# Turning an expert tile's rows by transposing DMAs instead of by PE transposes and an ACT copy

## The chip, the cores and the metric

The kernel runs on one core of one Trainium2 chip. The metric is the device time of one execution in microseconds. The kernel before takes 1347.95 us, the median of three runs (1347.94 to 1348.74).

## The reference, cut to what matters

The input is 16 images of 256 channels by 16 x 16 pixels. Two blocks follow each other. Each is a small gated or plain 1x1 convolution and then a mixture of experts over the 4096 pixels ("tokens") of 256 channels:

```python
# block 0, per token, over the top 2 of 8 experts (H = 512)
h = xf @ w1[e].T ;  g = xf @ w3[e].T ;  out += comb * ((silu(h) * g) @ w2[e].T)
# block 1, per token, over the top 2 of 8 experts (F = 1024)
h = silu(xf @ w1[e] + b1[e]) ;  out += comb * (h @ w2[e] + b2[e])
```

Both act on layer-normed tokens, and a router (a softmax over 8 logits) picks two experts for each token.

## The kernel before, in words

The kernel calls the two mixtures f = 0 and f = 1. Each is done sparsely. A token that chose expert e stands as one row in that expert's list; the lists are cut into tiles of 256 rows, so 8192 rows and their padding give 35 tiles here. Before a mixture the layer-normed rows are written to HBM (`rows_x`), each as 512 f16 numbers, 256 "high" parts and 256 "low" parts. `bounds[e]` holds the first tile of expert e; each engine loads all nine of its values into registers (`value_load`) and runs a loop per expert from `edges[e]` to `edges[e+1]`.

Around one tile n the engines do this:

* **POOL** (`feed_experts`, lines 446 to 494): `fetch_next` copies the list of row numbers and issues two indirect gathers (line 432), each bringing 128 rows to `x_rows`, [128 tokens, 512] f16. `put` copies the list of targets and issues two indirect scatters (line 471) of `y_rows` to HBM. `after(n, ...)` is a loop of one pass, written so that a wait can use the loop's own counter.
* **PE** (`experts`, line 718): `up` multiplies the tile's columns `x_cols` (channels on the partitions) by the expert's first weights, 48 matmuls of 256 columns for either f. `down` multiplies the activated result by the second weights, 24 matmuls in all for f = 0 (two calls of 12) and 48 for f = 1 (four calls of 12). Each product is formed from three f16 products (`PARTS`). Between the second-last and the last `down` stands `turn_rows(f, n + 1)` (line 675): 8 PE transposes of 128 x 128 f16 that turn the next tile's `x_rows` into a PSUM bank.
* **ACT** (line 869) applies Silu, makes the f16 parts for f = 0, and in `columns16` (line 863) copies the turned bank into `x_cols`, one instruction of 1024 columns a tile. For f = 0 it also moves the output to `y_rows`.
* **DVE** multiplies, forms the low parts and, for f = 1, moves the output to `y_rows`. For f = 0 it also finds, after each expert, the peaks of one expert's weights of mixture 1 (`scan1_peaks`), which lie in `scan1`.
* **SP** issues the loads of those weights, `load_scan`, two of 1 MB for each expert (lines 308 and 310): two experts' weights as soon as mixture 0's own weights are in place (`w_lo[0]`), then one more each time that DVE has finished one (`scanned`).

`x_rows` and `x_cols` exist once each. The order is kept by semaphores: `xr_loaded` (rows gathered), `xr_turned` (the bank is turned, which also frees `x_rows`), `xc_ready` (columns in place), `z_ready` (an `up` half is done, four a tile), `y_copied` and `y_free` (output moved, output stored). As the PE turns the next tile only after the last `up` of this one, `x_cols` is free when ACT writes it.

Of the kernel before, what the change touches and what calls it, by code (L numbers as in the profile page):

```python
# [24 lines left out]
ALU = mybir.AluOpType  # L25
# [3 lines left out]
F16 = mybir.dt.float16  # L29
# [21 lines left out]
def bass_metaformer(nc, x, conv_w, conv_b, gn_w, gn_b, gate0, w1, w2, w3, weight, bias,  # L51
                    gate1, gate1_b, v1, b1, v2, b2, out):
    ctx = ExitStack()
    with ctx:
# [214 lines left out]
        v1_scaled, v1_lo, fac_ready = sem("v1_scaled"), sem("v1_lo"), two("fac_ready")  # L269
        xr_loaded, xr_turned, xc_ready = two("xr_loaded"), two("xr_turned"), two("xc_ready")  # L270
        z_ready, silu_done, hid_ready, hi_ready, lo_ready = two("z_ready"), two("silu_done"), sem("hid_ready"), two("hi_ready"), two("lo_ready")
# [7 lines left out]
        def _(sp):  # L279
# [94 lines left out]

            sp.wait_ge(moves_ready[1], 1)
            total = sp.value_load(bounds[0:1, E:E + 1], min_val=E, max_val=TILES)
            sp.wait_ge(y_free[1], 32 * total + 16)
# [5 lines left out]
        def _(pool):  # L383
# [44 lines left out]

            def fetch(f, row_lists):

                for g_ in range(2):
                    nc.gpsimd.indirect_dma_start(x_rows[:, g_, :], None, rows_x[f],  # L432
                                                 bass.IndirectOffsetOnAxis(ap=row_lists[g_], axis=0)
                                                 ).then_inc(xr_loaded[f], 16)

# [10 lines left out]
            def feed_experts(f):  # L446


                if f == 0:
                    pool.wait_ge(peak_ready, E)  # L450
                    spread_peaks(0)
                pool.wait_ge(moves_ready[f], 1)
                pool.wait_ge(rows_stored[f], 16 * HB)
                total = pool.value_load(bounds[0:1, E:E + 1], min_val=E, max_val=TILES)
                fetch(f, [first_rows[:, g_:g_ + 1] for g_ in range(2)])
# [24 lines left out]

                fetch_next(0)
                with pool.Fori(0, total) as n:
                    fetch_next(n + 1)
                    put(n)

                def all_done(m):
                    pool.wait_ge(xc_ready[f], m + 2)
                    pool.wait_ge(xr_loaded[f], 32 * m + 96)
# [39 lines left out]
        def _(pe):  # L528
# [143 lines left out]

            x_turn16 = turn[0][:].bitcast(F16).rearrange("p (k s n) -> p k s n", k=KC, s=2)

            def turn_rows(f, tile):

                pe.wait_ge(xr_loaded[f], 32 * (tile + 1))
                for k in range(KC):
                    for s_ in range(2):
                        for r in range(2):  # L680
                            last = pe.transpose(x_turn16[:, k, s_, r * P:(r + 1) * P],  # L681
                                                x_rows[:, r, s_ * C + k * P:s_ * C + (k + 1) * P], ident16[:])
                last.then_inc(xr_turned[f], 1)

            PARTS = ((0, 0), (0, 1), (1, 0))

            def up(f, e, h):

                ws = ((w1_s, zb[2 * (h % 2)]), (w3_s, zb[2 * (h % 2) + 1])) if f == 0 else ((v1_s, zb[h]),)
                for w, z in ws:  # L690
                    for c in (2 * h, 2 * h + 1):
                        to = z[:, (c % 2) * TILE:(c % 2 + 1) * TILE]
                        for k in range(KC):
                            for ws_, xs_ in PARTS:
                                last = pe.matmul(to, w[:, e, k, ws_, c * P:(c + 1) * P], x_cols[:, k, xs_, :],  # L695
                                                 start=(k == 0 and ws_ + xs_ == 0), stop=(k == KC - 1 and ws_ == 1))
                    last.then_inc(z_ready[f], 1)
# [20 lines left out]
            def experts(f):  # L718
# [20 lines left out]
                if f == 1:  # L739
                    pe.wait_ge(xc_ready[1], edges[E] + 1)  # L740

# [48 lines left out]
        def _(act):  # L790
            def deviation(s):
                act.wait_ge(var_ready[s], 1)
                r, v = (rstd[:], var[:]) if s < 4 else (rstd_gn, var_gn)
                act.activation(r, v, ACT.Sqrt).then_inc(sd_ready[s], 1)

# [66 lines left out]

            def columns16(f, tile):

                act.wait_ge(xr_turned[f], tile + 1)
                act.activation(x_cols.rearrange("p k s n -> p (k s n)"), turn[0][:].bitcast(F16), ACT.Copy  # L866
                               ).then_inc(xc_ready[f], 1)

            def experts(f):
                halves = FH[f] // (2 * P)  # L870
                columns16(f, 0)
                edges = [act.value_load(bounds[0:1, e:e + 1], min_val=0, max_val=TILES) for e in range(E + 1)]
                act.wait_ge(fac_ready[f], 1)
                for e in range(E):
                    with act.Fori(edges[e], edges[e + 1]) as n:
                        for h in range(halves):
# [9 lines left out]
                            else:  # L886
# [75 lines left out]
        def _(dve):  # L962
# [8 lines left out]
            def deviations(s, count, eps):  # L971
# [8 lines left out]
                chain(dve.scalar_tensor_tensor(b[0], b[2], 1.0 / count, b[3], ALU.mult, ALU.add))  # L980
                dve.tensor_scalar(v, b[0], eps, None, ALU.add).then_inc(var_ready[s], 1)
                dve.wait_ge(sd_ready[s], 1)
                chain(dve.reciprocal(b[1], r))
# [479 lines left out]
```

## Time and profile before

| | us |
|---|---|
| median of 3 runs | 1347.95 |
| span of the profiled execution | 1347.4 |
| PE busy (share of the span) | 978.5 (73%) |
| DVE busy | 867.6 (64%) |
| ACT busy | 586.7 (44%) |
| POOL busy | 444.0 (33%) |
| expert tiles of f = 0, first to last `up` | 359.5 to 653.6 |
| expert tiles of f = 1, first to last `up` | 905.4 to 1284.7 |

The span runs from the first to the last instruction of the profiled execution; the page gives no other time for it. The rows name buffers by the tensor that holds them: `region` holds `x_rows`, `x_cols` and `y_rows`, `wreg` the weights, `bank` is PSUM, `routed` the lists. PEld is the loading of weights into the PE, which overlaps the matmuls. SPq rows are instructions of SP that issue a DMA: their length is the issue, not the transfer.

### The profile page before, as it was taken

The page shows a single profiled execution, that of the slowest core. Times are in us where ns is not written, and L with a number is a line of the kernel's source. Part 1 is how long each engine was busy: PE and PEld are TensorE (multiplying, and loading weights), DVE is VectorE, ACT ScalarE, POOL GpSimd, SP SyncE. Part 2 cuts the span into 40 slices and gives each one's busy share as a digit, 9 for nine tenths or more (in the row PEclk, how much of TensorE's full clock was granted, in tenths as well). Part 3 has the DMA queues.
Part 4 walks back from the last instruction along what each step waited for, and adds up shares of the span by engine and source line. Part 5 has one row for each costly group of instructions (what it writes and reads, how often), then busy time and mean ns, then how long its engine had stood idle before and what let it go on. Part 6 is the DMA issues. An engine that isn't in the chain of part 4 may idle for free.

```text
span 1347.4 us, 24878 instructions
## 1 busy us (share of the span) xinstructions
PE 978.5 (73%) x7761; PEld 830.6 (62%) x7761; DVE 867.6 (64%) x1854; ACT 586.7 (44%) x1055; POOL 444.0 (33%) x486
## 2 busy tenths in 40 slices
PE   5210667556699999999502669349999999999943
PEld 4100457426588888888401559128888888888832
DVE  6999689897454455555599885844555555545545
ACT  5200223275465555555524434455444444444422
POOL 1385000000055555555342540013444444444420
PEclk8655795558799999999855875559999999999965
DMA  7000007707522333332384302011111111111148
GB/s 227 1 0 0 0 1 249 250 0 241 180 96 92 125 125 125 125 121 67 124 265 161 109 32 94 16 47 35 49 49 47 51 51 48 47 47 47 47 145 260
DMA packets 88924, 127.80 MB, mean 95 GB/s; under 512 B 7920, under 2 KB 71864, under 8 KB 88760
## 3 DMA queue, kind: packets, MB, share of 16 engines
q1 hardware_dynamic: 70536, 84.34, 19.2%
q0 software_dynamic: 14000, 38.82, 8.8%
q10 hardware_dynamic: 4352, 4.20, 1.0%
q8 instruction: 18, 0.29, 0.1%
q14 instruction: 18, 0.15, 0.0%
HBM read 96.39 MB, written 30.93 MB: 94 GB/s over the span
## 4 chain that ended last, share of the span: by engine, by line
PE 58%; DVE 19%; issue 9%; DMA 7%; ACT 4%; DVEq 1%; POOL 1%; ACTq 0%; SPq 0%; POOLq 0%
PE bank L695 24%; PE bank L713 19%; PE bank L619 4%; PE bank L536 3%; PE bank L681 2%; DMA rows_y<-region,put_now 2%; DMA wreg<-rows_y 2%; DVE region L1031 2%; DVE tok L1372 2%; PE bank L755 2%; ACT xt L860 2%; DVE xt L1043 2%; DVE tok L1377 2%; PE bank L591 1%; DMA wreg<-in_L_ffn_w_dram 1%
## 5 line engine op out<-in xcount | busy, mean ns | idle before, releaser
L695 PE MATMUL bank<-region,wreg 128*128 128x256 f16 x3360 | 383.2, 275 | 11.0 <-issue 11.0
L695 PEld LDWEIGHTS bank<-region,wreg 128*128 128x128 f16 x3360 | 328.0, 99 | 55.0 <-issue 11.4
L713 PE MATMUL bank<-wreg,region 128*128 128x256 f16 x2520 | 298.2, 273 | 1.1 <-DVE region L1346 0.7
L713 PEld LDWEIGHTS bank<-wreg,region 128*128 128x128 f16 x2520 | 242.3, 98 | 31.0 <-DVE region L1346 2.7
L889 ACT ACTIVATE region<-bank,b_t,fac 128x256 f32<-128x256 f32 x280 | 142.9, 560 | 87.4 <-PE bank L695 84.0
L471 POOL DMA_INDIRECT rows_y<-region,put_now x140 | 150.7, 1076 | 87.8 <-issue 45.9
L432 POOL DMA_INDIRECT region<-rows_x,fetch_now x144 | 141.9, 986 | 92.9 <-POOL fetch_now L477 62.8
L1342 DVE SCALAR_TENSOR_TENSOR region<-bank,fac,region 128x256 f32<-128x256 f32 x140 | 61.3, 479 | 148.1 <-PE bank L695 80.5
L536 PE MATMUL bank<-ident,xn 128*128 128x128 f32 x256 | 57.0, 385 | 114.1 <-DVE xn L1002 106.6
L866 ACT ACTIVATE region<-bank 128x1024 f16<-128x1024 f16 x72 | 73.7, 1024 | 135.3 <-PE bank L681 135.1
L536 PEld LDWEIGHTS bank<-ident,xn 128*128 128x128 f32 x256 | 46.2, 209 | 123.0 <-DVE xn L1002 112.8
L1349 DVE TENSOR_SCALAR region<-region,fac 128x512 f16<-128x512 f32 x140 | 68.0, 486 | 79.6 <-ACT region L889 73.9
L1352 DVE SCALAR_TENSOR_TENSOR region<-region,fac 128x512 f16<-128x512 f32 x140 | 105.2, 751 | 5.0
L1357 DVE SCALAR_TENSOR_TENSOR region<-bank,fac,region 128x512 f32<-128x512 f32 x35 | 26.3, 751 | 117.0 <-PE bank L713 117.0
L477 POOL COPY fetch_now<-routed 128x2 uint32 (+1 forms) x72 | 13.6, 189 | 247.5 <-PE bank L681 247.5
L884 ACT ACTIVATE region<-region 128x256 f16<-128x256 f32 x140 | 56.6, 417 | 77.3 <-DVE region L1342 49.3
L619 PEld LDWEIGHTS bank<-gate_w,xt 128*128 128x128 f32 x256 | 55.8, 330 | 16.6 <-issue 16.1
L619 PE MATMUL bank<-gate_w,xt 128*128 128x8 f32 x256 | 57.1, 361 | 10.8 <-DVE st_lg L1148 10.8
L644 PE MATMUL bank<-xt,xn 128*128 128x160 f16 x128 | 39.4, 314 | 34.4 <-ACT xt L860 33.4
L1002 DVE TENSOR_SCALAR xn<-tok,mean,rstd 128x256 f32 (+1 forms) x128 | 60.1, 528 | 4.6 <-PE bank L536 2.5
L1346 DVE TENSOR_TENSOR region<-region 128x256 f16<-128x256 f32 x140 | 57.2, 425 | 6.4
L432 POOL DMA_INDIRECT region<-rows_x,first_rows x4 | 4.4, 1097 | 153.0 <-issue 153.0
(240 smaller groups left out, 1365.5 us busy)
## 6 DMA issues: line engine op xcount, KB each, us to landing
wreg<-in_L_ffn_w_dram SPq DMA_DIRECT2D x48, 512.0 KB, 5.9
wreg<-in_L_ffn_w_dram SPq DMA_DIRECT2D x16, 1024.0 KB
wreg<-rows_y SPq DMA_DIRECT2D x48, 256.0 KB, 3.7
region<-in_L_ffn_w_dram SPq DMA_DIRECT2D x12, 1024.0 KB, 7.4
rows_x<-region SPq DMA_DIRECT2D x16, 512.0 KB, 3.1
wreg<-in_x_dram SPq DMA_DIRECT2D x4, 1024.0 KB, 9.7
out_dram<-xt ACTq DMA_DIRECT2D x16, 256.0 KB, 3.6
region<-rows_x,fetch_now POOLq DMA_INDIRECT x144
```

The lines of the kernel that those rows point to most:

```text
L432: nc.gpsimd.indirect_dma_start(x_rows[:, g_, :], None, rows_x[f], bass.IndirectOffsetOnAxis(ap=row_lists[g_], axis=0)).then_inc(xr_loaded[ ...
L471: nc.gpsimd.indirect_dma_start(rows_y[f], bass.IndirectOffsetOnAxis(ap=put_now[:, g_:g_ + 1], axis=0), y_rows[:, g_, :], None).then_inc(y_ ...
L536: last = pe.transpose(to[:, k, h * P:(h + 1) * P], xn[:, j, h, k * P:(k + 1) * P], ident[:])
L619: last = pe.matmul(zb[j][:, h * E:(h + 1) * E], xt[:, j, k, h * P:(h + 1) * P], gate_w[:, f, k], start=(k == 0), stop=(k == KC - 1))
L695: last = pe.matmul(to, w[:, e, k, ws_, c * P:(c + 1) * P], x_cols[:, k, xs_, :], start=(k == 0 and ws_ + xs_ == 0), stop=(k == KC - 1 and ...
L713: last = pe.matmul(yb[:, r * C:(r + 1) * C], lhs[:, c, r * P:(r + 1) * P], w[:, e, c, ws_, :], start=first, stop=end, skip_group_check=True)
L866: act.activation(x_cols.rearrange("p k s n -> p (k s n)"), turn[0][:].bitcast(F16), ACT.Copy).then_inc(xc_ready[f], 1)
L889: last = act.activation(gate_act[:, h, c * TILE:(c + 1) * TILE], zb[h][:, c * TILE:(c + 1) * TILE], ACT.Silu, bias=b1_t[:, e, 2 * h + c:2 ...
L1002: last = dve.tensor_scalar(xn[:, j, h], tok[:, bass.ds(t, 1), :].rearrange("p a b -> p (a b)"), mean[:, bass.ds(t, 1)], rstd[:, bass.ds(t, ...
L1342: dve.scalar_tensor_tensor(half(hid[:, h], c), half(zb[2 * h + 1], c), fac[:, 1, e:e + 1], half(gate_act[:, h], c), ALU.mult, ALU.mult).th ...
L1349: dve.tensor_scalar(to_hi, gate_act[:, h], fac[:, 1, e:e + 1], None, ALU.mult).then_inc(hi_ready[f], 1)
L1352: dve.scalar_tensor_tensor(to_lo, gate_act[:, h], fac[:, 1, e:e + 1], to_hi, ALU.mult, ALU.subtract).then_inc(lo_ready[f], 1)
```

## The change

The PE transposes, the ACT copies and the semaphore `xr_turned` go. SP turns the rows instead, with two `dma_start_transpose` for each tile, one for each 128 rows, from SBUF to SBUF. `x_cols` keeps its address and is laid out by halves of rows (r) first; `up` reads it as two pieces of 128 columns. `xr_loaded` and `xc_ready` are now one semaphore for each half and f. SP waits until the tile's `up` is done (`z_ready`), then for each half waits for its gather, in a loop of one pass, and issues the DMA. POOL fetches the next half when `xc_ready` of that half has risen, in a loop of one pass for each. SP's loads of mixture 1's weights move into the loop over the experts: `load_scan(e + 1)` after expert e's tiles, once `scanned` is e. The `turn_rows` for the tile behind the last one stays. Ten semaphores of the norms become two that count in the order of use; who waits for what stays the same there.

```diff
-        x_cols = region[:, 4608:5120].bitcast(F16).rearrange("p (k s n) -> p k s n", k=KC, s=2)
+        x_cols = region[:, 4608:5120].bitcast(F16).rearrange("p (r s k n) -> p r s k n", r=2, s=2, k=KC)
...
-        var_ready = [sem(f"var_ready{s}") for s in range(5)]
-        sd_ready = [sem(f"sd_ready{s}") for s in range(5)]
+        var_ready, sd_ready = sem("var_ready"), sem("sd_ready")
+        norm_order = {0: 1, 4: 2, 1: 3, 2: 4, 3: 5}
...
             for e in range(2):
                 load_scan(e)
-            for e in range(E - 2):
-                sp.wait_ge(scanned, e + 1)
-                load_scan(e + 2)
-
-            total = sp.value_load(bounds[0:1, E:E + 1], min_val=E, max_val=TILES)
+            def turn_rows(f, n):
+                for r in range(2):
+                    with sp.Fori(n, n + 1) as m:
+                        sp.wait_ge(xr_loaded[r][f], 16 * m + 16)
+                    sp.dma_start_transpose(x_cols[:, r].rearrange("p s k n -> p (s k) n"), x_rows[:, r]).then_inc(xc_ready[r][f], 16)
+
+            def turn_tiles(f):
+                sp.wait_ge(moves_ready[f], 1)
+                edges = [sp.value_load(bounds[0:1, e:e + 1], min_val=0, max_val=TILES) for e in range(E + 1)]
+                turn_rows(f, 0)
+                for e in range(E):
+                    with sp.Fori(edges[e], edges[e + 1]) as n:
+                        sp.wait_ge(z_ready[f], 4 * n + 4)
+                        turn_rows(f, n + 1)
+                    if f == 0 and 1 <= e < E - 1:
+                        sp.wait_ge(scanned, e)
+                        load_scan(e + 1)
+                return edges[E]
+
+            total = turn_tiles(0)
+            for r in range(2):
+                sp.wait_ge(xc_ready[r][0], 16 * total + 16)
             sp.wait_ge(y_free[0], 32 * total + 16)
...
-            def fetch(f, row_lists):
-                for g_ in range(2):
-                    nc.gpsimd.indirect_dma_start(x_rows[:, g_, :], None, rows_x[f], ...
-                                                 ).then_inc(xr_loaded[f], 16)
+            def fetch(f, r, row_list):
+                nc.gpsimd.indirect_dma_start(x_rows[:, r, :], None, rows_x[f], ...
+                                             ).then_inc(xr_loaded[r][f], 16)
...
                 def fetch_next(n):
-                    pool.wait_ge(xr_turned[f], n + 1)
+                    if not isinstance(n, int):
+                        for r in range(2):
+                            pool.wait_ge(xr_loaded[r][f], 16 * n + 16)
                     nc.gpsimd.tensor_copy(fetch_now[:], moves[:, bass.ds(2 * n, 2), 0]).then_inc(fetches_copied[f], 1)
                     after(n, lambda m: pool.wait_ge(fetches_copied[f], m + 1))
-                    fetch(f, [fetch_now[:, g_:g_ + 1] for g_ in range(2)])
+                    for r in range(2):
+                        after(n, lambda m: pool.wait_ge(xc_ready[r][f], 16 * m + 16))
+                        fetch(f, r, fetch_now[:, r:r + 1])
...
# PE: experts(f)
-                turn_rows(f, 0)
                 edges = [pe.value_load(...) for e in range(E + 1)]
                 for e in range(E):
                     with pe.Fori(edges[e], edges[e + 1]) as n:
-                        pe.wait_ge(xc_ready[f], n + 1)
+                        for r in range(2):
+                            pe.wait_ge(xc_ready[r][f], 16 * n + 16)
                         for h in range(halves):
                             up(f, e, h)
-                        for h in range(halves - 1):
+                        for h in range(halves):
                             down(f, e, n, h, halves)
-                        turn_rows(f, n + 1)
-                        down(f, e, n, halves - 1, halves)
...
# ACT: experts(f)
-                columns16(f, 0)
...
-                        columns16(f, n + 1)
```

## Rows read from the trace of the kernel before

**Rows 1.** The page: the span; the chain that ended last, by engine.
```profile
span 1347.4 us, 24878 instructions
PE 58%; DVE 19%; issue 9%; DMA 7%; ACT 4%; DVEq 1%; POOL 1%; ACTq 0%; SPq 0%; POOLq 0%
```

**Rows 2.** Chain of waits, one tile of f = 0: start us, us, what.
```profile
378.76 5.24 PE bank L695 x48
384.00 1.31 PE bank L713 x12
385.31 0.45 PE bank L681 x8
385.75 1.36 PE bank L713 x12
```

**Rows 3.** Timeline, f = 1: start us, us, engine, line, operation.
```profile
1268.50 5.40 PE L695 MATMUL bank<-region,wreg 128*128 128x256 f16 x48
...
1279.42 5.40 PE L695 MATMUL bank<-region,wreg 128*128 128x256 f16 x48
```

**Rows 4.** Timeline, f = 0: who wakes after the PE transposes, and POOL's work.
```profile
385.79 1.02 ACT L866 ACTIVATE region<-bank 128x1024 f16<-128x1024 f16 x1 [0.28 <-PE bank L681]
385.95 0.18 POOL L477 COPY fetch_now<-routed 128x2 uint32 x1 [1.61 <-PE bank L681]
386.96 5.40 PE L695 MATMUL bank<-region,wreg 128*128 128x256 f16 x48
387.06 1.00 POOL L432 DMA_INDIRECT region<-rows_x,fetch_now  x1 [0.92 <-POOL fetch_now L477]
388.37 0.96 POOL L432 DMA_INDIRECT region<-rows_x,fetch_now  x1 [0.30 <-issue]
```

**Rows 5.** DMA issues on SP: start us, us of the issue.
```profile
353.83 0.54 SPq L310 DMA_DIRECT2D wreg<-in_L_ffn_w_dram  x1
399.08 0.47 SPq L310 DMA_DIRECT2D wreg<-in_L_ffn_w_dram  x1
```

**Rows 6.** Landing: the gathers of `rows_x`; SP's stores; the scatters and loads of `rows_y`.
```profile
DMA to landing us min/median/max: 2.9/3.1/4.8
rows_x<-region SPq DMA_DIRECT2D x16, 512.0 KB, 3.1
DMA to landing us min/median/max: 2.7/3.9/7.6
```

**Rows 7.** Start of f = 0; stretches (us, busy by engine, PEclk, DMA share, GB/s).
```profile
359.49 7.83 PE L695 MATMUL bank<-region,wreg 128*128 128x256 f16 x48 [5.71 <-issue]
364.00:366.00 2.00, 2.00 (x18) 1.72 (x17) 1.18 (x3) 0.75 (x2) 0.00 (x0) 0.88 1.00 315
366.00:368.00 2.00, 2.00 (x20) 1.80 (x19) 1.16 (x4) 0.86 (x3) 0.00 (x0) 1.00 0.01 2
```

**Rows 8.** Timeline, end of f = 0's tiles.
```profile
653.57 1.47 PE L713 MATMUL bank<-wreg,region 128*128 128x256 f16 x12
661.46 0.97 POOL L471 DMA_INDIRECT rows_y<-region,put_now  x1 [0.30 <-issue]
663.90 0.34 SPq L354 DMA_DIRECT2D routed<-in_L_conv_bias_dram  x1
```

**Rows 9.** Timeline, start of f = 1.
```profile
893.07 0.17 DVE L1270 TENSOR_SCALAR first_rows<-routed 128x2 uint32<-128x2 uint32 x1
899.12 1.01 PE L681 MATMUL bank<-ident,region 128*128 128x128 f16 x8 [8.06 <-DMA region<-rows_x,first_rows]
905.38 7.94 PE L695 MATMUL bank<-region,wreg 128*128 128x256 f16 x48 [5.25 <-issue]
```

**Rows 10.** Stretches elsewhere in the kernel, for the granted clock (columns as in rows 7).
```profile
760.00:770.00 10.00, 4.74 (x26) 3.93 (x27) 9.59 (x15) 4.87 (x4) 4.37 (x4) 1.00 0.11 36
345.00:352.00 7.00, 5.28 (x24) 4.98 (x24) 4.18 (x6) 4.12 (x6) 0.00 (x0) 0.58 0.00 0
345.21 1.01 PE L661 MATMUL bank<-ident,wreg 128*128 128x128 f32 x4 [4.13 <-DMA wreg<-in_L_ffn_w_dram]
```

More of the change, by code:

```diff
@@ L269, in bass_metaformer @@
         v1_scaled, v1_lo, fac_ready = sem("v1_scaled"), sem("v1_lo"), two("fac_ready")
-        xr_loaded, xr_turned, xc_ready = two("xr_loaded"), two("xr_turned"), two("xc_ready")
+        xr_loaded, xc_ready = ([two(f"{name}{r}_") for r in range(2)] for name in ("xr_loaded", "xc_ready"))
         z_ready, silu_done, hid_ready, hi_ready, lo_ready = two("z_ready"), two("silu_done"), sem("hid_ready"), two("hi_ready"), two("lo_ready")
@@ L373, in _ @@
                 store_rows(1, i)
-            sp.wait_ge(moves_ready[1], 1)
-            total = sp.value_load(bounds[0:1, E:E + 1], min_val=E, max_val=TILES)
+            total = turn_tiles(1)
+            for r in range(2):
+                sp.wait_ge(xc_ready[r][1], 16 * total + 16)
             sp.wait_ge(y_free[1], 32 * total + 16)
@@ L427, in _ @@
                 gate_by_columns(nc.gpsimd, r, k).then_inc(gated_by_pool, 1)
-            def fetch(f, row_lists):
-                for g_ in range(2):
-                    nc.gpsimd.indirect_dma_start(x_rows[:, g_, :], None, rows_x[f],
-                                                 bass.IndirectOffsetOnAxis(ap=row_lists[g_], axis=0)
-                                                 ).then_inc(xr_loaded[f], 16)
+            def fetch(f, r, row_list):
+                nc.gpsimd.indirect_dma_start(x_rows[:, r, :], None, rows_x[f],
+                                             bass.IndirectOffsetOnAxis(ap=row_list, axis=0)
+                                             ).then_inc(xr_loaded[r][f], 16)
             def after(n, waits):
@@ L454, in feed_experts @@
                 total = pool.value_load(bounds[0:1, E:E + 1], min_val=E, max_val=TILES)
-                fetch(f, [first_rows[:, g_:g_ + 1] for g_ in range(2)])
+                for r in range(2):
+                    fetch(f, r, first_rows[:, r:r + 1])
                 to, bias_of = ((gate_b[:], gate1_b), (b2_all, b2))[f]
@@ L474, in fetch_next @@
                 def fetch_next(n):
-                    pool.wait_ge(xr_turned[f], n + 1)
+                    if not isinstance(n, int):
+                        for r in range(2):
+                            pool.wait_ge(xr_loaded[r][f], 16 * n + 16)
                     nc.gpsimd.tensor_copy(fetch_now[:], moves[:, bass.ds(2 * n, 2), 0]).then_inc(fetches_copied[f], 1)
                     after(n, lambda m: pool.wait_ge(fetches_copied[f], m + 1))
-                    fetch(f, [fetch_now[:, g_:g_ + 1] for g_ in range(2)])
+                    for r in range(2):
+                        after(n, lambda m: pool.wait_ge(xc_ready[r][f], 16 * m + 16))
+                        fetch(f, r, fetch_now[:, r:r + 1])
                 fetch_next(0)
@@ L486, in all_done @@
                 def all_done(m):
-                    pool.wait_ge(xc_ready[f], m + 2)
-                    pool.wait_ge(xr_loaded[f], 32 * m + 96)
+                    for r in range(2):
+                        pool.wait_ge(xr_loaded[r][f], 16 * m + 48)
                     pool.wait_ge(y_free[f], 32 * m + 48)
@@ L671, in stage_turns @@
                         last.then_inc(w_turned, 1)
[L673 to L683, printed above, removed]
             PARTS = ((0, 0), (0, 1), (1, 0))
@@ L694, in up @@
                             for ws_, xs_ in PARTS:
-                                last = pe.matmul(to, w[:, e, k, ws_, c * P:(c + 1) * P], x_cols[:, k, xs_, :],
+                                last = pe.matmul(to, w[:, e, k, ws_, c * P:(c + 1) * P], x_cols[:, :, xs_, k, :],
                                                  start=(k == 0 and ws_ + xs_ == 0), stop=(k == KC - 1 and ws_ == 1))
@@ L729, in experts @@
                     with pe.Fori(edges[e], edges[e + 1]) as n:
-                        pe.wait_ge(xc_ready[f], n + 1)
+                        for r in range(2):
+                            pe.wait_ge(xc_ready[r][f], 16 * n + 16)
                         for h in range(halves):
                             up(f, e, h)
-                        for h in range(halves - 1):
+                        for h in range(halves):
                             down(f, e, n, h, halves)
-                        turn_rows(f, n + 1)
-                        down(f, e, n, halves - 1, halves)
-                if f == 1:
-                    pe.wait_ge(xc_ready[1], edges[E] + 1)
             routing(0)
@@ L791, in deviation @@
             def deviation(s):
-                act.wait_ge(var_ready[s], 1)
+                act.wait_ge(var_ready, norm_order[s])
                 r, v = (rstd[:], var[:]) if s < 4 else (rstd_gn, var_gn)
-                act.activation(r, v, ACT.Sqrt).then_inc(sd_ready[s], 1)
+                act.activation(r, v, ACT.Sqrt).then_inc(sd_ready, 1)
             def copy_images(i):
@@ L861, in route @@
                                        scale=id_f[:, b % 2, bass.ds(4 * i + b // 2, 1)]).then_inc(ids_listed, 1)
[L863 to L867, printed above, removed]
             def experts(f):
                 halves = FH[f] // (2 * P)
-                columns16(f, 0)
                 edges = [act.value_load(bounds[0:1, e:e + 1], min_val=0, max_val=TILES) for e in range(E + 1)]
@@ L980, in deviations @@
                 chain(dve.scalar_tensor_tensor(b[0], b[2], 1.0 / count, b[3], ALU.mult, ALU.add))
-                dve.tensor_scalar(v, b[0], eps, None, ALU.add).then_inc(var_ready[s], 1)
-                dve.wait_ge(sd_ready[s], 1)
+                dve.tensor_scalar(v, b[0], eps, None, ALU.add).then_inc(var_ready, 1)
+                dve.wait_ge(sd_ready, norm_order[s])
                 chain(dve.reciprocal(b[1], r))
```

## The prediction

> **What bounds the kernel now.** The page comes first. Its chain by engine gives PE 58% and DVE 19% [rows 1], a mean over stages of which the change touches only the two tile loops, so I read those. The chain of waits in f = 0 [rows 2] is all PE: `up` 5.24, a `down` 1.31, the turn of the next rows 0.45, the last `down` with its small gap 1.36, together 8.36 us a tile. PE waits for nothing in it; between the end of an `up` and the start of the next lie 1.31 + 0.45 + 1.36 = 3.12 us. In f = 1 a tile takes 1279.42 - 1268.50 = 10.92 us [rows 3], so 10.92 - 5.24 = 5.68 us lie between two `up`s. There are 35 tiles, thus 34 such stretches for each f.
>
> What the reader is to see: `x_cols` exists once. The next tile's columns can be written only after an `up` has ended, and the next `up` waits for them. Today this is done by 0.45 us of PE and 1.02 us of ACT [rows 4], and it hides under the last `down`. After the change the whole way SP, DMA, semaphore lies in that stretch. I call its length T, from the end of `up` to the start of the next.
>
> **What is removed.** 0.45 us of PE a tile, on the path: the stretch left to PE is 3.12 - 0.45 = 2.67 us in f = 0 and 5.68 - 0.45 = 5.23 in f = 1. The ACT copy is off the path; I count it as nothing.
>
> **What is added: T.** Step by step:
> - SP sees the semaphore. POOL wakes at 385.95 after a turn that ended at 385.31 + 0.45 = 385.76 [rows 2, 4]: 0.19.
> - The loop of one pass around the wait for the first half. POOL's gap before its first gather has such a loop, 0.92, the one before its second hasn't, 0.30 [rows 4]: 0.62. Bounds: 0 and 0.92.
> - Issue of the first DMA: 0.47, as a load's [rows 5]. Bounds: 0.47, and for an instruction that costs SP more, 1.5, between the issue of a gather (1.00 [rows 4]) and three loads.
> - The second loop: 0.62.
> - The second DMA, from issue to landing. No row shows a transposing DMA. The nearest by size is the gather of the same 128 KB into the same place: 3.1 at the median, 4.8 at most. Below it is SP's store of 512 KB, also 3.1 [rows 6]; taking off 384 KB at the 315 GB/s of [rows 7] leaves 1.9. Above it is the slowest move of `rows_y`, 7.6 [rows 6]. I take 3.1.
> - PE wakes: ACT's copy ends at 386.81, `up` starts at 386.96 [rows 4]: 0.15.
>
> T = 0.19 + 0.62 + 0.47 + 0.62 + 3.1 + 0.15 = 5.15 us.
>
> In f = 0 this is longer than 2.67, so the stretch grows from 3.12 to 5.15: 34 x 2.03 = +69.0 us. In f = 1 it just fits under the 5.23 of `down`: 34 x -0.45 = -15.3 us; there the cover ends at T = 5.23, and each 0.1 us beyond costs 3.4 us.
>
> The Trainium skill ("VectorE: DVE Perf Modes", section on the three transpose paths) gives 390 ns for a 128 x 128 bf16 transpose on TensorE and 1309 ns for one by the DMA crossbar, and advises TensorE where PSUM will do. The trace agrees with the first only as a bound, with eight in 0.45 us; no run here shows the second. As an estimate from that page: if the four blocks of one DMA went at once, T would be 3.36 and the time 1350; if one after another, 5.2 instead of 3.1, T would be 7.25 and the time 1551. It speaks against the change either way.
>
> **Is another loop longer?** The first half lands at T - 0.62 - 0.47 - 0.15 = 3.9 after `up`. POOL then needs 0.19 and issues the gathers (1.00, a new loop 0.92, 0.96 [rows 4]); the second starts at 6.0 and lands at 9.1. SP wants it at 5.24 + 5.15 + 0.19 + 0.62 + 0.47 + 0.62 = 12.3, so 3.2 us are left, and POOL's own round (about 8 us of gathers and scatters) fits into 10.4. The queue behind SP's waits is only its own `load_scan`; its instructions go after the tile's DMAs. PE's two pieces of 128 columns in place of one of 256 I take as free (bounds: none shown), likewise the merged semaphores of the norms, where the same engine waits for the same event.
>
> **Start of f = 0.** SP issues 4 MB of loads until 353.83 + 0.54 = 354.37 [rows 5], then loads nine bounds into registers (PE's took 5.7 us [rows 7]) and issues the DMAs at 360 to 362. The loads run until 366: 315 GB/s in the last two us, 2 after it [rows 7]. The DMAs are issued on the same queue. If they wait for it, they land near 366 + 1.5, half a landing, and `up` starts at 367.5, not 359.49: +8. If they go beside the loads, 363.5: +4; if they begin only at 366, 369.3: +10. I take +8.
> The Trainium skill ("DMA: Bandwidth & Descriptors", section on queues, rings and completion order) says that on each DMA engine what SP issues is consumed in ring order, which is the +8; sharing would be the +4. No run here shows it.
>
> **Loads inside f = 0.** Six times 2 MB follow a tile's two DMAs, issued about 3 us after `up`. At 315 GB/s they last 6.7 us, until about 10, just before the next tile's DMAs at 11.2. They slow gathers (4.8 instead of 3.1, within the 3.2 us left) and scatters (7.6 instead of 3.9 [rows 6]). 0 to 8 us; I take +2.
>
> **Ends and the start of f = 1.** The last scatters of f = 0 come after POOL's fetch, which now waits for the DMA: 3.9 + 0.19 + 1.00 + 0.92 + 0.96, then copy 0.2, loop 0.92, scatter 1.0 and gap 0.30, so the second starts 9.4 after `up` and lands 663.90 - 661.46 = 2.4 later, 11.8. Before it was 663.90 - 653.57 = 10.3 [rows 8]: +1.5. The end of f = 1 I take as unchanged: its last `down` is longer and covers more of POOL's fetch. At the start of f = 1, PE today turns at 899.12, when the rows have landed, and only then loads its bounds until 905.38 [rows 9]. Now it loads them earlier; SP loads its own from 893.3 to about 899, and the second half lands near 903: -2.1 (-3 to -1).
>
> **Sum.** 69.0 - 15.3 + 8 + 2 + 1.5 - 2.1 = +63.1. From the span of 1347.4, 1410.5; the median of the runs stands 0.55 above the span, so 1411. For another T the time is 1347.95 + 34 (T - 3.12) + 34 max(-0.45, T - 5.68) + 9.4.
>
> **The rivals.**
> - The DMAs are slower than a gather, or SP takes long to issue them (T of 6.2 to 8). Speaks for it: a transpose moves f16 numbers, not rows of 1 KB. Against: it stays in SBUF. At T = 7: 34 x 3.88 + 34 x 1.32 + 9.4 = +186, 1534.
> - The PE clock falls too. Before a stretch of granted clock 0.58 the PE had sat idle 4.13 us [rows 10], and a first `up` after idling takes 7.83 instead of 5.40 [rows 4, 7]: 2.43 more. In f = 0 the idle part is T - 2.67, so it comes in from T = 6.8 on: 173 + 34 x 2.43 = +255, 1603. Against it at T = 5.15: a stretch with PE busy 4.74 of 10 us kept clock 1.00 [rows 10], and here 7.9 of 10.4 are busy.
> - A middling case, T of 3.4 to 4.3, with the lower landing of 1.9 us: at 4.0, 34 x 0.88 - 15.3 + 9.4 = +24, 1372.
> - The other side: the way is hidden. Landing 1.9, loops of 0.1: T = 2.91, the start +4: -7.1 - 15.3 + 5.4 = -17, 1331. It decides at T = 3.29. For it: PE's 0.45 is certainly saved. Against: no DMA in [rows 6] lands under 2.7.
> - The change gains and loses alike, T within 0.08 of 3.29: 1348. That the DMA doesn't turn whole rows but moves single numbers would make T tens of us; I leave it outside.
>
> **Chances.** Forecast (T of 4.3 to 6.2) 0.50, its own range 1382 to 1480; slower DMAs 0.22; with the clock 0.08; middling 0.12; hidden 0.06; alike 0.02. Range: from T = 4.0, 1372, to T = 7.5, 1568. What a measurement can tell from no change is 0.2%, 2.7 us. Faster 0.06, same 0.02, slower 0.92.
>
> **What would show it.** After: `up` in f = 0 every 10.4 us with PE idle near 2.5 before each, the releaser a DMA into `region`; in f = 1 every 10.47 without idle; first `up` near 367.5 and, in f = 1, 2 us sooner after the lists than now; no L681 or L866 rows; PEclk still 1.0 in the tile loops. Wrong it would be if `up` followed `up` in f = 0 within 8.4 us, or if f = 1 too showed PE idle before each tile.

## The result: 4.6% slower, and the profile after

The changed kernel takes 1410.27 us (median of 4 runs, 1408.85 to 1415.1) where the kernel before takes 1348.35 on the same chip (1347.94 to 1350.27): a ratio of 1.0461 [1.0442, 1.048]. The prediction said 1411, with 0.92 for slower. The total is right. Inside T, the way from the end of one `up` to the start of the next, the issue of a DMA was taken too short and its landing too long, and the two made up for each other; the loads inside f = 0 cost more than predicted. That is what the experiments are about.

The page of the changed kernel, its head, clock, packets and the chain by engine:

```profile
span 1407.9 us, 25218 instructions
PE 954.9 (68%) x7185; PEld 793.1 (56%) x7185; DVE 870.9 (62%) x1854; ACT 515.9 (37%) x983; POOL 443.9 (32%) x486
...
PEclk9655875568799999999995587555999999999975
...
DMA packets 167262, 146.69 MB, mean 104 GB/s; under 512 B 86256, under 2 KB 150200, under 8 KB 167096
...
PE 49%; DVE 18%; DMA 15%; issue 8%; SPq 5%; ACT 3%; DVEq 1%; ACTq 0%; POOLq 0%; POOL 0%
```

Against the kernel before, PE has lost 23.6 us of busy time and ACT 70.8, and yet the span is 60.5 longer: the work went away and a wait came. DMA is now 15% of the chain that ended last. The groups say where the wait is:

```profile
L709 PE MATMUL bank<-region,wreg 128*128 128x256 f16 x3360 | 386.4, 276 | 90.2 <-DMA region<-region 90.2
...
L727 PE MATMUL bank<-wreg,region 128*128 128x256 f16 x2520 | 292.6, 273 | 15.2 <-DVE region L1345 15.2
...
region<-region SPq DMA_TRANSPOSE x144, 2.4
```

PE idles 90.2 us before `up` (L709), all of it ended by a DMA from `region` to `region`; this is the new one, 144 of them, 2.4 us from issue to landing.

**One tile of f = 0.** The chain of waits, answering to [rows 2] (start, length, what; "SPq L353" is the loop around the wait for the rows, "SPq L355" the issue of a transposing DMA):

```profile
381.82 0.09 SPq L353
...
382.17 0.04 issue
382.21 1.19 SPq L355
383.40 0.04 issue
383.45 0.03 SPq L353
...
383.73 0.04 issue
383.77 2.41 DMA region<-region
386.18 0.14 issue
386.32 5.71 PE bank L709 x48
```

and PE's timeline over the same tile (start, busy, what, and in brackets the idle time before it and what ended it):

```profile
376.12 5.40 PE L709 MATMUL bank<-region,wreg 128*128 128x256 f16 x48 [1.63 <-DMA region<-region]
...
381.36 1.47 PE L727 MATMUL bank<-wreg,region 128*128 128x256 f16 x12
...
383.28 1.48 PE L727 MATMUL bank<-wreg,region 128*128 128x256 f16 x12 [0.45 <-DVE region L1345]
```

A tile takes 386.32 - 376.12 = 10.20 us, so T = 10.20 - 5.24 = 4.96. Predicted were 10.4 and 5.15. In PE's timeline the idle time before `up` is only 1.6, not 2.5. Another 0.45 stands before the second `down`, which waits for DVE.

**f = 1.** PE's timeline, answering to [rows 3]:

```profile
1298.23 5.40 PE L709 MATMUL bank<-region,wreg 128*128 128x256 f16 x48
1303.47 5.40 PE L727 MATMUL bank<-wreg,region 128*128 128x256 f16 x48
1308.71 3.55 PE L709 MATMUL bank<-region,wreg 128*128 128x256 f16 x31
```

10.48 us a tile (predicted 10.47, before 10.92), and no idle time: T of 4.96 fits under the 5.24 of `down`.

**Start of f = 0.** SP's timeline, with the first two transposing DMAs:

```profile
357.69 3.34 SPq L355 DMA_TRANSPOSE region<-region  x2
```

The last of the four loads ahead of them, to be read against 353.83 in [rows 5]:

```profile
351.56 0.61 SPq L311 DMA_DIRECT2D wreg<-in_L_ffn_w_dram  x1
```

Stretches of 2 us at the end of the loads (the last three columns are granted clock, DMA share, GB/s):

```profile
362.00:364.00 2.00, 0.00 (x0) 0.00 (x0) 0.00 (x0) 0.00 (x0) 0.00 (x0) 0.50 1.30 252
364.00:366.00 2.00, 1.17 (x6) 0.87 (x7) 0.00 (x0) 0.00 (x0) 0.83 (x1) 0.50 0.04 3
```

And the first `up` in PE's timeline:

```profile
364.83 6.69 PE L709 MATMUL bank<-region,wreg 128*128 128x256 f16 x48 [17.85 <-DMA region<-region]
```

The DMAs are out at 361.0, and `up` starts only when the 4 MB of loads have stopped, at 364.83 against 359.49 before. That is +5.3, but the loads were issued 2.3 us sooner in this execution. Over the runs of this case the first of them goes out between 348.7 and 354.3, and in two kernels with the same code up to there (the one before and one_turn below) at 352.3 and 350.4, so I take it for spread between executions. Counted from the loads, `up` comes 7.6 us later than before. waits_first below, whose loads go out when those of the kernel before do, has its first `up` at 366.93, +7.4.

**Three tiles of f = 0** of the 34 after the first look like the one below, with PE idle 2.50, 3.15 and 3.88 us before them. Each follows a load:

```profile
612.72 7.07 PE L709 MATMUL bank<-region,wreg 128*128 128x256 f16 x48 [2.50 <-DMA region<-region]
```

The chain of waits ahead of it says what was late, and the stretch of 2 us inside it gives the granted clock (third from the end):

```profile
600.84 7.14 DMA region<-rows_x,fetch_now
...
610.13 2.45 DMA region<-region
...
614.00:616.00 2.00, 2.00 (x11) 1.40 (x10) 0.00 (x0) 0.69 (x1) 1.11 (x3) 0.50 0.22 66
```

The late one is a gather of the rows, issued beside the load of 600.43: 7.1 us from issue to landing here, 8.3 and 8.0 in the other two tiles, where one beside no load took 3.0 (366.48 to 369.45). The transposing DMA behind it took its usual 2.4. Then PE runs at a granted clock of 0.50, and `up` takes 7.07.

The whole +60.5 us of the span, by the starts of `up`:

| part | measured, us | predicted |
|---|---|---|
| first `up` of f = 0 (+7.6 counted from the loads' issue) | +5.3 | +8 |
| f = 0, 34 x (10.20 - 8.36) | +62.6 | +69.0 |
| f = 0, tiles longer than that (4.6 before, 11.8 after) | +7.1 | +2 (0 to 8) |
| from the last `up` of f = 0 to the first of f = 1 | +0.8 | -0.6 |
| f = 1, its 34 tiles | -15.1 | -15.3 |
| behind the last `up` | -0.2 | 0 |
| sum | +60.5 | +63.1 |

### The profile page after: what moved, and what is told of

It is laid out like the page before. It is cut to its first block, busy times and chain, and to the rows that moved or that the text cites. A ratio compares the mean times of both kernels' runs of the same rounds, so it can differ in the third digit from the quotient of the medians.

```text
span 1407.9 us, 25218 instructions
## 1 busy us (share of the span) xinstructions
PE 954.9 (68%) x7185; PEld 793.1 (56%) x7185; DVE 870.9 (62%) x1854; ACT 515.9 (37%) x983; POOL 443.9 (32%) x486
## 2 busy tenths in 40 slices
DMA packets 167262, 146.69 MB, mean 104 GB/s; under 512 B 86256, under 2 KB 150200, under 8 KB 167096
## 4 chain that ended last, share of the span: by engine, by line
PE 49%; DVE 18%; DMA 15%; issue 8%; SPq 5%; ACT 3%; DVEq 1%; ACTq 0%; POOLq 0%; POOL 0%
PE bank L709 25%; PE bank L727 12%; DMA region<-region 7%; PE bank L645 4%; DMA region<-rows_x,fetch_now 3%; SPq L355 3%; PE bank L562 2%; DMA wreg<-rows_y 2%; DVE region L1030 2%; DVE tok L1371 2%; PE bank L762 2%; ACT xt L867 2%; DVE xt L1042 1%; DMA wreg<-in_L_ffn_w_dram 1%; PE bank L617 1%
## 5 line engine op out<-in xcount | busy, mean ns | idle before, releaser
L709 PE MATMUL bank<-region,wreg 128*128 128x256 f16 x3360 | 386.4, 276 | 90.2 <-DMA region<-region 90.2
L709 PEld LDWEIGHTS bank<-region,wreg 128*128 128x128 f16 x3360 | 330.0, 99 | 141.3 <-issue 64.0
L727 PE MATMUL bank<-wreg,region 128*128 128x256 f16 x2520 | 292.6, 273 | 15.2 <-DVE region L1345 15.2
L493 POOL DMA_INDIRECT rows_y<-region,put_now x140 | 142.3, 1017 | 84.6 <-issue 71.2
L880 ACT ACTIVATE region<-bank,fac 128x512 f32<-128x512 f32 x70 | 48.1, 687 | 92.7 <-PE bank L709 92.7
L846 ACT ACTIVATE xt<-bank 128x512 f32<-128x512 f32 x48 | 28.5, 594 | 53.4 <-PE bank L562 53.4
```

The source lines that it names most:

```text
L727: last = pe.matmul(yb[:, r * C:(r + 1) * C], lhs[:, c, r * P:(r + 1) * P], w[:, e, c, ws_, :], start=first, stop=end, skip_group_check=True)
```

## The experiments

My theory after the result: the loss is T in f = 0, and nothing else of size. T is made of SP's own time (wake, loops, issue) and the landing; the loads beside it add some microseconds. A clean tile is one of the usual length of that kernel. "Excess" below is the time from the first to the last `up` of f = 0 less 34 clean tiles of that kernel.

**More T: one more transposing DMA a tile.**

```diff
+                    if r == 0:
+                        sp.dma_start_transpose(spare, x_rows[:, 0]).then_inc(xc_ready[0][f], 16)
                     sp.dma_start_transpose(x_cols[:, r]..., x_rows[:, r]).then_inc(xc_ready[r][f], 16)
```

> One more transposing DMA of 128 KB into an unused place, issued ahead of the first half of each tile; POOL and PE wait for it with the first half. Theory: T grows by one issue, 1.19 + 0.04: f = 0 +1.23 x 34 = +42, and f = 1, whose cover is 5.24, is uncovered: T 6.2, +0.95 x 34 = +32: 1484. If the PE clock also falls once PE idles about 2.8 us before each up (as it did after the tiles 612.7, 656.8 and 701.6, whose up took 7.07 instead of 5.40), f = 0 loses another 1.67 x 34 = 57: 1541. Rival (the DMAs are hidden in f = 1 whatever they take, or the landing and not the issue counts): f = 1 stays at 10.48 and the time at most 1452.

1512.49 us, 1.1225 [1.1185, 1.1266]. PE's timeline in f = 0:

```profile
442.94 5.41 PE L714 MATMUL bank<-region,wreg 128*128 128x256 f16 x48 [2.76 <-DMA region<-region]
...
454.45 7.08 PE L714 MATMUL bank<-region,wreg 128*128 128x256 f16 x48 [2.78 <-DMA region<-region]
...
467.27 5.41 PE L714 MATMUL bank<-region,wreg 128*128 128x256 f16 x48 [2.77 <-DMA region<-region]
```

The tile takes 454.45 - 442.94 = 11.51, so T rose by 1.31, not by a landing: what a DMA adds is its place on SP (1.19 of issue, 0.04 of gap, and 0.08 by which the next issue is longer). f = 1 now pays too, 11.51 a tile. In f = 0, 21 of the 34 `up`s took 7.08 in place of 5.41. That is where this run passes the first expectation, 1484: 21 x 1.31 = 28 us (the next tile is 12.82 later). The clock rival came true in part, at 2.8 us of idle; in the stretch 456 to 458 us the granted clock is 0.50.

**Less T: both waits for the rows before the wait for `up`.**

```diff
                     with sp.Fori(edges[e], edges[e + 1]) as n:
+                        wait_rows(f, n + 1)
                         sp.wait_ge(z_ready[f], 4 * n + 4)
+                        sp.sem_inc(sp_step, 1)
                         turn_rows(f, n + 1)        # now only the two DMAs
```

> SP waits for both gathers before z_ready and without loops of one pass; behind z_ready come one semaphore instruction and the two DMAs. Theory: T loses the two loops, 4.96 to about 4.3: f = 0 -0.66 x 34 = -22, f = 1 nothing, as T is under its 5.24 already: 1388, or 1383 if the three falls of the clock go too. Rival (the loops ran while SP waited for something else): no change, 1410.

1403.79 us, 1.0413 [1.0373, 1.0454], where 1388 was expected. PE's timeline:

```profile
446.31 5.40 PE L717 MATMUL bank<-region,wreg 128*128 128x256 f16 x48 [0.98 <-DMA region<-region]
...
455.97 5.40 PE L717 MATMUL bank<-region,wreg 128*128 128x256 f16 x48 [0.97 <-DMA region<-region]
```

A clean tile takes 9.66, T = 4.42: 0.54 less, which over 34 tiles should be 18 us. The time from first to last `up` of f = 0 fell by 6.0 only (358.55 to 352.52), because the excess rose from 11.8 to 24. Most of the excess is in six tiles beside the loads (11.4 to 12.6 us each, against 10.3 to 12.5 in the change), and in the tiles behind them, as five `up`s after the first ran slow in place of three. The chain of waits ahead of the longest but one:

```profile
456.77 6.70 DMA region<-rows_x,fetch_now
```

Again it is a gather beside a load that is late. So two thirds of the gain, 12 of 18 us, went back at those tiles. That the shorter clean tile is the reason, by leaving a slowed gather less time, fits this but no run shows it apart.

**The loads taken out.** The six loads inside f = 0 are left out (the peaks of the later experts come from the first two experts' weights).

```diff
                         sp.wait_ge(scanned, e)
-                        load_scan(e + 1)
```

> The six loads of 2 MB inside f = 0 are left out; the peaks of the other experts are taken of the first two experts' weights. Theory: the tiles of f = 0 that take more than 10.20 us (11.8 us too much in all, three of them followed by an up of 7.07) do so because the loads slow the gather and the transposes: all tiles at 10.20, no slow up, 1398. Rival (the change of expert itself, its loop's start on SP, costs it): the excess stays and the time is 1410.

1400.39 us, 1.0384 [1.0355, 1.0413]. f = 0 took 351.14, 7.4 less, the clean tile is still 10.20, and every `up` after the first took 5.40. The excess is 4.3, near the 4.6 of the kernel before. So the loads' term is 7 to 8 us, three slow `up`s (3 x 1.67 = 5.0) in it. It may be up to 9: the first `up` took 8.29 here and 6.69 in the change, a spread between executions that hides 1.6 of it.

**The loads issued by ACT.** Is it SP's queue that makes the DMAs late, or the DMA engines' time?

```diff
-                        load_scan(e + 1)           # SP
+                        act.dma_start(scan1[:, n_ % 2, 0]..., v1[E - 1 - n_]...)   # ACT, after expert e's tiles
+                        act.dma_start(scan1[:, n_ % 2, 1]..., v2[E - 1 - n_]...)
```

> The changed kernel, but the six loads of 2 MB inside f = 0 are issued by ACT, after its last instruction of the expert's tiles, and not by SP: another queue, the same 16 DMA engines. Theory (the transposes stand behind the loads in SP's own queue, so a tile beside a load is late by up to 2.3 us, and PE's clock falls): no tile of f = 0 much over 10.3, no up of 7.07: the excess of 11.8 us shrinks to 4 or less, 1402. Rival (the loads take the DMA engines' time, whoever issues them): excess and slow ups as before, 1410.

1407.36 us, 1.0446 [1.0407, 1.0486]; f = 0 took 357.87, the change 358.55. Still three slow `up`s, as PE's timeline shows:

```profile
552.29 5.40 PE L706 MATMUL bank<-region,wreg 128*128 128x256 f16 x48 [1.55 <-DMA region<-region]
563.89 7.07 PE L706 MATMUL bank<-region,wreg 128*128 128x256 f16 x48 [3.04 <-DMA region<-region]
```

The chain of waits ahead of the second:

```profile
551.52 8.08 DMA region<-rows_x,fetch_now
```

So another queue doesn't help. The gather, which POOL issues, is late beside a load, whether SP or ACT issued that load.

**The first tile turned before the first 4 MB of loads.**

```diff
-            sp.wait_ge(w_lo[0], 6 * E)             # these three lines now stand behind turn_rows(0, 0)
-            for e in range(2):
-                load_scan(e)
```

> SP turns tile 0 of f = 0 before it waits for the weights and issues the first 4 MB of loads; the rows have long been gathered by then. Theory (the first up, at 364.8 instead of 359.5, waits for DMAs issued behind 4 MB of loads in the same queue): the first up starts when PE has loaded its nine bounds, near 357.5: -7, 1403. Rival (the first up waits for PE's own loading of the bounds): start as now, 1410.

1400.47 us, 1.0389 [1.0359, 1.0419]. PE's timeline, to be read against 364.83 above:

```profile
358.62 6.83 PE L709 MATMUL bank<-region,wreg 128*128 128x256 f16 x48 [10.62 <-issue]
```

The first `up` comes 6.2 us sooner, 0.9 before that of the kernel before; PE then waits for its own bounds, no longer for a DMA. The rest of the gain (f = 0 took 353.14, 5.4 less) is one slow `up` after the first (7.07, at 462.84 us) in place of three, and a clean tile of 10.16.

**Two buffers for the columns.** `x_cols` gets two places, chosen by n & 1, so SP turns tile n + 1 while `up` n runs. To make room, other buffers of `region` move, and SP's one-pass loops around the waits become plain waits.

```diff
-        x_cols = region[:, 4608:5120]...("p (r s k n) -> p r s k n", r=2, s=2, k=KC)
+        x_cols = region[:, 7168:8192]...("p (j r s k n) -> p j r s k n", j=2, r=2, s=2, k=KC)
...
                     with sp.Fori(edges[e], edges[e + 1]) as n:
+                        turn_rows(f, n + 1, sp.snap((n + 1) & 1))
                         sp.wait_ge(z_ready[f], 4 * n + 4)
-                        turn_rows(f, n + 1)
```

> Theory (the one buffer x_cols puts the whole way SP, DMA, semaphore between two ups): with two buffers, used in turn, the transposes of tile n + 1 run during the up of tile n, so PE never waits for them. f = 0: a tile falls from 10.20 to 5.24 + 3.1 to 3.25, say 8.4 us (-61 us over 34), and the 11.8 us that the tiles beside the loads lose go with it; f = 1 stays at 10.48. The first up stays near 364.8. Sum 1410 - 61 - 10 = about 1339, under the kernel before. Rival (the DMAs' own traffic, or PE's matmuls with a register in their address, or the changed queues cost the time): f = 0 stays near 10.2 a tile and the time near 1410.

1345.57 us, 0.9975 [0.9956, 0.9995]: the whole 4.6% is gone. With that the cause is shown: not the DMA is dear, but the one address that holds it back until `up` has ended. The loops that went too can't be it, since waits_first without its two loops gained 0.54 a tile and this run 1.99. A clean tile takes 8.21 in f = 0 and 10.48 in f = 1. The expected 1339 was missed, as f = 0 has an excess of 20 us. PE's timeline:

```profile
563.39 5.40 PE L712 MATMUL bank<-region,wreg 128*128 x48
574.15 7.10 PE L712 MATMUL bank<-region,wreg 128*128 x48 [2.38 <-DMA region<-region]
```

Such tiles stand beside the loads. Whether a second `x_rows` as well would take away the excess wasn't tried. The same kernel **without the six loads**:

> Two buffers for the columns, and the six loads of 2 MB inside f = 0 left out (peaks taken of the first two experts' weights). Theory (the excess of 20 us over 34 tiles of 8.21 in f = 0 is the loads': gather, transpose and gather again are a loop of some 8 us on the single x_rows, without slack, which the loads stretch): all tiles near 8.21, 1346 - 18 = 1328. Rival (the loop itself, or the change of expert, costs it): 1346.

1335.05 us, 0.9897 [0.9867, 0.9927]; f = 0 took 286.66 in place of 299.12, no slow `up` after the first. The loads cost this kernel 12.5 of its 20 us. The theory had 1328 and put all 20 on them; the other 7.5 are not explained, but for 2.5 in the first tile.

**What was the PE turn worth?** In the kernel before, PE turns one block of eight (every tile after the first takes 7/8 of its columns from tile 0).

```diff
-                for k in range(KC):
-                    for s_ in range(2):
-                        for r in range(2):
+                for k in range(KC if isinstance(tile, int) else 1):       # the other two loops likewise
```

> The kernel before, but PE turns only one of the eight blocks for every tile after the first (the rest of the columns stays tile 0's); ACT copies as before. It shows what PE's turning was worth by itself. The prediction's step (0.45 us a tile on the path in f = 0 and in f = 1 alike; here seven eighths, 0.39): -13 for each f, 1322. Rival (in f = 0 the turn stands in a wait for DVE's low part, which starts the second down 1.94 us after the first without it against 1.78 with it): f = 1 -13, f = 0 at most -5, 1330.

1357.2 us, 1.0066 [1.0039, 1.0092], against both theories. The replaced columns of f = 0 change the routing of f = 1, which has 37 tiles here in place of 35; the two more are 21 us, so the total says nothing and only the stages can be read. In f = 1 the tile takes 10.53, 0.39 less, as 7/8 of 0.45 says. In f = 0 the time from first to last `up` is 288.73, before 288.84: nothing gained. The tiles are of two kinds, twelve of 8.21 to 8.25 and seventeen, in a row, of 8.53 to 8.59. PE's timeline of one of the second kind:

```profile
451.47 5.40 PE L695 MATMUL bank<-region,wreg 128*128 128x256 f16 x48
456.71 1.47 PE L713 MATMUL bank<-wreg,region 128*128 128x256 f16 x12
458.02 0.22 PE L681 MATMUL bank<-ident,region 128*128 128x128 f16 x1
458.70 1.48 PE L713 MATMUL bank<-wreg,region 128*128 128x256 f16 x12 [0.47 <-DVE region L1346]
```

The second `down` now waits 0.47 for DVE. In the first kind it waits 0.12, and 0.15 of the tile's 8.36 is saved. With all of the turn gone, two_bufs has 8.21 too. So of its 0.45 at least 0.30 filled a wait that was there anyway, and in the second kind all of it.

**One DMA of 256 KB for the tile**, with both waits first:

```diff
-                for r in range(2):
-                    sp.dma_start_transpose(x_cols[:, r]..., x_rows[:, r]).then_inc(xc_ready[r][f], 16)
+                sp.dma_start_transpose(x_cols[:]..., x_rows.rearrange("p g c -> p (g c)")).then_inc(xc_ready[0][f], 16)
```

> As the run with the waits first, but one transposing DMA of 256 KB a tile in place of two of 128 KB. The issue of one took SP 1.19 us where a load takes 0.47. Theory (SP issues a transpose block by block, so the issue grows with its size): issue near 2.3, T near the 4.4 of the waits-first run, time 1404 (1400 to 1408). Rival (1.19 is a fixed price of the instruction): T 3.3, f = 0 about 8.7 a tile, 1372.

1388.62 us, 1.029 [1.0261, 1.0318], between the two theories. The chain of waits:

```profile
441.23 0.02 SPq L372
441.25 0.05 issue
441.30 3.94 DMA region<-region
445.24 0.14 issue
```

The issue takes 1.24 us at the median, near the 1.19 of 128 KB: from 128 to 256 KB it hardly grows. But the landing takes 3.94 where the second DMA of waits_first takes 2.48, so T is 4.3, against 4.42 there, and nearly all that the saved issue (1.23) and a shorter wake of SP (0.2 in place of 0.5) give is lost again. Only in f = 0 is the landing that long. Over all 72 DMAs of the run the median is 3.1, as in f = 1 nearly all take 3.04:

```profile
DMA to landing us min/median/max: 2.7/3.1/6.6
```

Why f = 0 adds 0.9 stays open. f = 0 took 338.71, 13.8 less than waits_first. The clean tile gives under 4 of that; the other 10 are the excess, 14 us in place of the 24 of the kernel with two DMAs and the same order of waits.

**Two versions meant to be best.** Two buffers, the first tile turned ahead of the loads, and PE's bounds loaded before it waits for the weights' factors; the first also with the loads on ACT.

> Two buffers for the columns, the six loads issued by ACT, tile 0 turned before the first loads, PE's nine bounds loaded before it waits for the weights. Theory: first up near 357 instead of 365; 34 tiles of 8.21 with an excess of 5 us, not 20, in f = 0; 10.48 in f = 1. From the 1345.6 of the two buffers alone, -8 and -15: 1322, under the kernel before. Rival (the transposes' traffic slows gathers and scatters whoever issues the loads): excess as with two buffers alone, 1337.

1349.74 us, 1.0006 [0.9983, 1.0029], against both theories. The first `up` was at 351.71, but f = 0 took 312.24, 33 us over 34 clean tiles, most of it beside the loads. PE's timeline:

```profile
632.92 5.40 PE L709 MATMUL bank<-region,wreg 128*128 x48
645.62 7.08 PE L709 MATMUL bank<-region,wreg 128*128 x48 [3.91 <-DMA region<-region]
```

On ACT's queue the loads do more harm here than on SP's, by the two ratios 1.1%. The chain of waits ahead of this `up`:

```profile
634.76 10.51 DMA region<-region
```

This time the late one is the transposing DMA itself, issued 1 us after a load of ACT's: 10.5 us to landing in place of 2.4. With SP's queue, in the next run, it is again the gather (8.2 us) and the transposing DMA takes 2.4. Back on SP's:

> Two buffers for the columns, tile 0 turned before the first loads, PE's nine bounds loaded before it waits for the weights; the six loads stay in SP's queue. Theory: the start 8 us sooner than with two buffers alone, the excess in f = 0 still 20: 1338, under the kernel before by 0.7%. Rival (an earlier start only lets the first loads stretch the first tiles): 1346.

1337.53 us, 0.9897 [0.9867, 0.9926], where 1338 was expected: f = 0 starts at 357.14 (its loads went out 5.6 us later than those of the run before, within the spread named above) and takes 298.66. By the two ratios this is 0.8% under the version with two buffers alone, and 1.0% under the kernel before: the fastest of those that compute everything.

## Why the prediction was right

**T: right as a sum, its terms not.** Predicted 0.19 + 0.62 + 0.47 + 0.62 + 3.1 + 0.15; the chain above has 0.46 (from the next `down`'s start at 381.36) + 0.39 + 1.19 + 0.37 + 2.41 + 0.14. The issue was taken as a load's [rows 5] and costs 2.5 times that, though within the bound of 1.5: +0.72. The landing is 0.69 shorter, the two loops together 0.48, and the wake is 0.27 longer. That the sum is right to 0.2 us is luck. POOL's loop [rows 4] is no measure for SP's, which takes two fifths less.

The 3.1 for the landing rests on a misread row. What [rows 6] calls the landing of the gathers, 2.9/3.1/4.8, is that of SP's 16 stores of 512 KB, the same as the line below it; the scatters' 7.6 is the slowest of SP's loads of `rows_y`. The list of issues of the kernel before gives no landing for a gather:

```profile
region<-rows_x,fetch_now POOLq DMA_INDIRECT x144
```

That a gather beside no load takes 3.0 (see the three tiles above) is a coincidence with those 3.1. Of the 0.19 for the wake: in the chain above it is 0.46 and with one DMA 0.19 (441.04 to 441.23); why stays open. That the tile is 5.24 + T was tested from both sides: extra_dma has 11.51 in f = 0 and in f = 1, past the cover (T of 6.27), and waits_first 9.66 in f = 0 (T of 4.42) and no gain in f = 1, under it (359.06 us from first to last `up`, the change 358.96).

The Trainium skill ("VectorE: DVE Perf Modes", section on the three transpose paths) gives 1309 ns for one 128 x 128 block by the DMA crossbar. The trace has 2.41 us for four, which lies between all at once and one after another. The page's advice to leave such turns to TensorE where PSUM will do holds here with one buffer (ratio 1.0461); with two the ways are within 0.5% of each other (0.9975).

**f = 0: 2.03 a tile predicted, 1.84 measured.** The mechanism is confirmed by two_bufs. One reading in it was wrong: "the stretch left to PE is 2.67 us". It subtracts the turn from a stretch in which the second `down` would then wait for DVE; one_turn shows that at most 0.15 of the 0.45 comes free. As T decided the tile, it had no effect on the forecast. It would have misled with the way hidden: 8.36 - 0.45 is 7.91 a tile, and two_bufs reached 8.21.

**f = 1: right**, -0.45 a tile with T under the cover of 5.24; there PE is the bound and its turn was worth all of its 0.45.

**Start of f = 0: +5.3 for +8.** SP had its bounds at 357.69, not 360 to 362, and the loads stopped at 364, not 366, both because this execution issued the loads 2.3 us sooner; counted from them it is +7.6, and the term was right. The DMAs land as the loads stop, and first_early (-6.2) shows that `up` waited for them. The Trainium skill ("DMA: Bandwidth & Descriptors", section on queues, rings and completion order) says that each DMA engine consumes the descriptors of one ring in order, and the trace agrees. Sharing with loads that end at the same time would look alike, so the two aren't told apart.

**Between the stages: +0.8 for -0.6.** The end of f = 0 is as predicted: from the last `up` to POOL's first work behind the last scatter 15.8 us before and 17.0 after, +1.2 for +1.5. At the start of f = 1, `up` comes 11.16 us after the lists (12.31 before), -1.15 for -2.1. The rest, 0.7, lies between and was not looked into.

**Loads inside f = 0: mis-sized.** +2 predicted, +7.1 measured, within the 0 to 8. The step that failed is "they slow gathers (4.8 instead of 3.1, within the 3.2 us left)". The 4.8 was a store's. The gathers ahead of the three slow tiles took 7.1 to 8.3 us, 4 to 5 more than one beside no load, so they ran past the slack and held up SP. The idle time then brought the clock term, which makes about 5 of the 7.1. The transposing DMAs hardly slow there (3.8 us at the most beside one of the six loads, 2.4 at the median); their 6.6 is the first one of f = 0, behind the 4 MB.

**The total** was predicted to 1 us by luck too: -6.4 in the tiles of f = 0, -2.7 at the start, +5.1 by the loads and +1.4 between the stages make the span 2.6 shorter than predicted, and the median stands 2.4 above the profiled span, not 0.55.

**The clock.** The forecast said full clock at T of 5.15 and a fall from T = 6.8 on. At T = 4.96 it held (granted clock 1.00 at 480 to 500 us) but for three tiles, whose stretch was longer; at T = 6.27 it fell in 21 of 34. The bound was too high; it came from a single idle stretch of 4.13 us [rows 10], and the shortest idle time before a slow `up` of these runs is 2.35 us (loads_act).

## What to carry to other kernels

A DMA that writes the only copy of a buffer costs its whole chain (wake, loops, issue, landing) between the last reader and the next; move it there only if that stretch is longer than the chain, or give it a second buffer first. Before you count an engine's removed time as saved, look whether the next instruction on that engine already waits for another: then it is a filler. A gain on a tile loop can be partly given back at the tiles beside large loads, as 12 of 18 us were here, so cost these tiles by themselves. And look whether a view's landing time belongs to the instruction you mean: a view by buffer mixes all that touch it.

## What the hardware showed that was not expected

* A transposing DMA takes SP 1.19 us to issue for 128 KB and 1.24 for 256 KB, where a load inside f = 0 takes 0.4 to 0.5. Landing from the start of the issue: 2.4 for 128 KB; for 256 KB 3.0 in f = 1 and 3.9 in f = 0.
* A gather of 128 KB that lands in 3.0 us took 6.7 to 8.3 beside a load of 2 MB, whether SP or ACT had issued the load. A transposing DMA issued 1 us after a load on ACT's queue took 10.5 in place of 2.4.
* A transposing DMA cuts its transfer small: packets under 512 B rose from 7920 to 86256 with 144 such DMAs, and the bytes moved by 18.9 MB.
* `up` fell to the lower clock (7.07 in place of 5.40 us) after 2.35 to 2.5 us of idle in some tiles (loads_act, two_bufs, the change) and stayed at 5.40 after 2.77 in others (extra_dma); here it was not a matter of one idle stretch alone.
* A one-pass loop costs SP 0.37 to 0.39 us.
